# Experts stage: expert outputs with features on partitions, three of four pieces in high and low parts, blocks overlapped, square-root chains per token

## What is computed

```python
q = elu(x @ Wq.T + bq) + 1; k = elu(x @ Wk.T + bk) + 1; v = x @ Wv.T + bv
kv = einsum('nshd,nshm->nhmd', k, v)
z = 1.0 / einsum('nlhd,nhd->nlh', q, k.sum(axis=1) + 1e-6)
ctx = einsum('nlhd,nhmd,nlh->nlhm', q, kv, z)
hs = ctx @ Wd.T + bd + x
attn = (hs - mean(hs)) / sqrt(var(hs) + 1e-12) * gamma + beta
...
top_w, top_idx = top_k(x @ W_gate, 2); combine = one_hot(top_idx) * softmax(top_w)
for e in range(8):
    h = gelu(x @ W_in[e] + b_in[e])            # 128 -> 512
    out = out + combine[..., e, None] * (h @ W_out[e] + b_out[e])   # 512 -> 128
x = x + attn + out
```

## Time and profile before

| | us |
|---|---|
| median of 3 runs | 4531.86 (4531.02 to 4533.04) |
| profiled execution | 4536.7 |
| its span | 4534.8 |
| PE busy | 4234.2 (93%) |
| DVE busy | 3704.0 (82%) |
| ACT busy | 3133.7 (69%) |
| experts_phase | from about 3900 to the end |

### The profile page before, as it was taken

One profiled execution on the slowest core, in us unless ns is written; L12 is line 12 of the kernel. 1 busy time (PEld: TensorE's weight loads), 2 busy tenths in 40 slices (PEclk: granted clock), 3 DMA queues, 4 the chain that ended last, 5 costly groups with the idle time before them and its releaser, 6 DMA issues. The chain is left out here.

```text
span 4534.8 us, 117827 instructions
## 1 busy us (share of the span) xinstructions
PE 4234.2 (93%) x44769; PEld 3395.3 (75%) x44769; DVE 3704.0 (82%) x6460; ACT 3133.7 (69%) x4912; POOL 1783.8 (39%) x965
## 2 busy tenths in 40 slices
PE   6888599999999999999999999999999999599999
PEld 2434278887888878888788887888788888387888
DVE  6888788888888888888888888888888887565553
ACT  5888477777777777777777777777777777243333
POOL 0000155555555555555455555555555554000000
PEclk9999799999999999999999999999999999699999
DMA  2111132232323232322332233322233223100000
GB/s 82 43 43 43 41 69 65 69 72 64 85 68 73 65 83 68 73 68 64 84 73 69 66 68 81 75 67 66 69 81 78 65 65 72 47 8 9 5 7 5
DMA packets 343226, 271.55 MB, mean 60 GB/s; under 512 B 231320, under 2 KB 236064, under 8 KB 341536
## 3 DMA queue, kind: packets, MB, share of 16 engines
q1 hardware_dynamic: 342688, 264.25, 24.3%
HBM read 29.23 MB, written 4.19 MB: 7 GB/s over the span
## 5 line engine op out<-in xcount | busy, mean ns | idle before, releaser
L679 POOL TENSOR_TENSOR qk_rotated<-qk_rotated,rotary_sines 128x1024 f32<-128x1024 f32 x384 | 924.3, 2407 | 1497.7 <-DVE rotary_sines L761 1497.7
L690 POOL TENSOR_TENSOR qk_rotated<-qk_rotated,rnorm 128x1024 f32<-128x1024 f32 x384 | 733.6, 1911 | 7.4
L769 DVE TENSOR_REDUCE qk_sumsq<-qk_squared 128x16 f32<-128x1024 f32 x384 | 465.7, 1213 | 91.7 <-ACT qk_squared L516 91.7
L230 PE MATMUL ps_proj<-qkv_w_hi,x_shifted_hi 128*128 128x512 f32 x1152 | 512.1, 445 | 18.5 <-DVE rotary_sines L761 11.6
L523 ACT ACTIVATE q_t<-ps_qk_t 128x512 f32<-128x512 f32 x384 | 229.7, 598 | 406.5 <-PE ps_qk_t L286 397.6
L751 DVE TENSOR_TENSOR qk_rotated<-ps_proj,rotary_scaled 128x1024 f32<-128x1024 f32 x384 | 467.6, 1218 | 4.5 <-ACT qk_squared L516 4.2
L761 DVE TENSOR_TENSOR rotary_sines<-ps_proj,rotary_scaled 128x1024 f32<-128x1024 f32 x384 | 467.1, 1216 | 1.4 <-POOL qk_rotated L679 1.4
L232 PE MATMUL ps_proj<-qkv_w_hi,x_shifted_lo 128*128 128x512 f32 x1152 | 460.2, 399 | 0.0
L537 ACT ACTIVATE k_t_by_head<-ps_qk_t 64x512 f32<-64x512 f32 x768 | 451.0, 587 | 10.4 <-PE ps_qk_t L295 0.9
L231 PE MATMUL ps_proj<-qkv_w_lo,x_shifted_hi 128*128 128x512 f32 x1152 | 456.4, 396 | 0.0
L311 PE MATMUL ps_scores<-k_t_by_head,q_t 128*32 128x128 f32 x12288 | 415.1, 276 | 9.7 <-ACT ps_scores L546 5.2
(11 more groups left out here) (260 smaller groups left out, 9699.5 us busy)
## 6 DMA issues: line engine op xcount, KB each, us to landing
v_by_window<-v_tokens SPq DMA_DIRECT2D x1152, 128.0 KB, 2.4
v_by_window<-v_tokens SPq DMA_DIRECT2D x384, 64.0 KB, 2.0
k_t_by_head<-k_t_by_head SPq DMA_DIRECT2D x96, 256.0 KB, 4.3
v_by_window<-v_by_window SPq DMA_DIRECT2D x192, 64.0 KB, 2.0
qkv_w_raw<-in_layer_qk_dram SPq DMA_DIRECT2D x7, 1664.0 KB, 9.1
f_k_stacked<-f_k_hi SPq DMA_DIRECT2D x64, 64.0 KB, 2.0
f_k_stacked<-f_k_lo SPq DMA_DIRECT2D x64, 64.0 KB, 2.0
f_q_stacked<-f_q_hi SPq DMA_DIRECT2D x64, 64.0 KB, 2.0
```

The source lines that it names most:

```text
L230: mm(out, hi, HI[:, o:o + 512], start=True, stop=False)
L679: tt(u, u, TB[:], ALU.add).then_inc(added, 1)
L690: tt(u, u, r.unsqueeze(3).broadcast_to((P, 2, 8, DH)), ALU.mult).then_inc(scaled, 1)
L769: nc.vector.reduce_sum(SS[:, 16 * i:16 * i + 16], SQ[:].rearrange("p (h e) -> p h e", e=DH), AX).then_inc(sumsq, 1)
```

## The change

1. Expert output with features on partitions: `expert(i, e, m)` now takes piece m of the 512 hidden features, with w_out stationary and the hidden piece (512 tokens) moving. For m < HS_ = 3 it is three fp32r products of high and low parts; the fourth piece (m = 3) is one fp32 product. ACT makes the high part HHI of each hidden piece one slot later (`high_hidden`), DVE the low part HLO two slots later (`low_hidden`); PE uses piece t four slots later. w_out is split too (WOHI by ACT at t = 14 of block 0, WOLO by DVE in turn 0).
2. The combine weight is now needed along the free axis. CT (8 x 512) is saved to DRAM and read back as eight rows, each broadcast to 128 partitions, into CB, which lies on WI. DVE multiplies (`weigh`, into TMP) and adds (`add`, into Y), both 128 x 512, once per expert. All rows go over SP's queue, one at a time.
3. The bias products are two (KB, slot 5). Y is turned back into tokens by four transposes into VB at t = 7 of the next turn (`tokens_out`), copied by ACT at t = 8 and stored.
4. Turns overlap: pieces 0 and 1 of expert 7 close the turn, 2 and 3 run in slots 2 and 3 of the next one; the last two weightings are at t = 0 and 4 there. `high_x(i + 1)` runs at t = 31. `drain` ends the last turn.
5. Norms: a product with CENT = I - 1/128 centres directly; ACT squares and copies from PSUM; the variance is four products with one column (MCOL), tokens on partitions, so that the 12 steps of the chain work on 128 x 4; DVE multiplies by the identity (`rstd_diag`, 128 x 512) and PE spreads it with a product with ONES. For the second norm W_d and b_d are folded with CENT once at the start (WDC, BDC), and CENT x XN is accumulated under it, in place of the residual. Gamma and beta move to ACT (t = 27), as does q's max (a Relu at t = 10).
6. The combine weights are made in four steps over all chunks in place of eight.

The core of the diff:

```diff
+            def spread_row(i, e):
+                landed, made = held(16 * (E_ * i + e)), held(16 * i + 16)
+                if not isinstance(i, int) or i > 0:
+                    read = held(E_ * (i - 1) + e + 1)
+                    sp.wait_ge(weighted, read)
...
+                after(sp, cb_in, landed)
...
+                sp.dma_start(CB[:, e, :], saved[e:e + 1, :].broadcast_to((P, BLK))).then_inc(cb_in, 16)
...
             with sp.Fori(1, NBLK - 1) as i:
...
+                load_x(i + 1)
+                rows(i, 5, E_)
+                store(i - 1)
+                save_combine(i + 1)
+                rows(i + 1, 0, 5)
...
+            def variance(n):
+                pe.wait_ge(sq, n + 1)
+                for c in range(NT):
+                    last = mm(KV[:, c:c + 1], ZQ[:, chunk(c)], MCOL[:], start=True, stop=True)
...
+            def spread_rstd(n, bank):
+                pe.wait_ge(diag, n + 1)
+                mm(bank[:], ONES[:], DG[:].rearrange("p c d -> p (c d)"), start=True, stop=True).then_inc(spread, 1)
...
+                    mm(G[:], CENT[:], XN[:], start=True, stop=False)
                     pe.wait_ge(ctx_done, i + 1)
-                    mm(G[:], W[:, C_WD:C_WD + P], CTX[:], start=True, stop=True).then_inc(wd_mm, 1)
+                    mm(G[:], WDC[:], CTX[:], start=False, stop=True).then_inc(centered, 1)
...
+            def expert(i, e, m):
+                if m == 0:
+                    after(pe, y_acc, E_ * i + e - 1)
+                if m < HS_:
+                    pe.wait_ge(lo_out, HS_ * (E_ * i + e) + m + 1)
+                    b = e % 2
+                    mm(YB[b][:], WOHI[:, e, m, :], HHI[:, b, m, :], start=(m == 0), stop=False)
+                    mm(YB[b][:], WOHI[:, e, m, :], HLO[:, b, m, :], start=False, stop=False)
+                    last = mm(YB[b][:], WOLO[:, e, m, :], HHI[:, b, m, :], start=False, stop=(m == HM - 1))
+                else:
+                    pe.wait_ge(h_out, SLOTS * i + HM * e + m + 1)
+                    last = mm(YB[e % 2][:], WO[:, e, m, :], HL[:, e % 2, m - HS_, :], start=False, stop=(m == HM - 1))
...
                     if e > 0:
-                        expert(e - 1, m)
+                        expert(i, e - 1, m)
+                    elif m >= 2 and not first:
+                        expert(i - 1, E_ - 1, m)
+                    if t == 5:
...
+                        mm(KB[:], IDENT[:], AT[:], start=True, stop=False)
+                        mm(KB[:], BO[:], CT[:], start=False, stop=True).then_inc(y0_mm, 1)
+                    if t == 7 and not first:
+                        tokens_out(i - 1)
...
-                for c in range(NT):
-                    expert(E_ - 1, c)
-                pe.wait_ge(y_acc, SLOTS * (i + 1))
+                for m in range(2):
...
+                    expert(i, E_ - 1, m)
...
+            def high_hidden(i, e, m):
+                act.wait_ge(h_out, SLOTS * i + HM * e + m + 1)
+                after(act, e_mm, E_ * i + e - 1)
+                a(HHI[:, e % 2, m, :], H[:, m, :], ACT.Copy).then_inc(hi_out, 1)
...
+                    if m < HS_:
+                        after(act, lo_out, HS_ * (E_ * i + e - 1) + m + 1)
...
+                    if t > 0 and (t - 1) % HM < HS_:
+                        high_hidden(i, (t - 1) // HM, (t - 1) % HM)
...
+            def low_hidden(i, e, m):
+                dve.wait_ge(hi_out, HS_ * (E_ * i + e) + m + 1)
+                tt(HLO[:, e % 2, m, :], H[:, m, :], HHI[:, e % 2, m, :].bitcast(F32), ALU.subtract).then_inc(lo_out, 1)
+
+            def weigh(i, e):
+                dve.wait_ge(e_mm, E_ * i + e + 1)
+                dve.wait_ge(cb_in, 16 * (E_ * i + e + 1))
+                after(dve, y_acc, E_ * i + e)
+                tt(TMP[:], YB[e % 2][:], CB[:, e, :], ALU.mult).then_inc(weighted, 1)
...
                     e, m = t // HM, t % HM
+                    if t >= 2 and (t - 2) % HM < HS_:
+                        low_hidden(i, (t - 2) // HM, (t - 2) % HM)
```

More of the change, by code:

```diff
@@ L1585, in _ @@
             tail_sum(q)
[L1588 to L1645, removed]
 def XF2(XF, i):
@@ L1717, in experts_phase @@
[L1717 to L1721, removed]
+        NUM, DEN = KB, VB
+        w_in_s, x_in, x_out, experts_in, cd_in, cb_in = (sem(x) for x in ("weights_in", "x_in", "x_out", "experts_in", "combine_saved", "combine_in"))
@@ new lines, in save_combine, with load_x, store @@
+            def save_combine(i):
+                made, landed = held(i + 1), held(16 * E_ * i)
+                sp.wait_ge(ct_out, made)
+                after(sp, cb_in, landed)
+                sp.dma_start(saved, CT[:]).then_inc(cd_in, 16)
+            def load_x(i):
+                summed = held(i)
+                sp.wait_ge(x1_done, summed)
+                sp.dma_start(XA[:], x_attn[:, i, :]).then_inc(x_in, 16)
+            def store(i):
+                evicted = held(i + 1)
+                sp.wait_ge(yo_out, evicted)
+                sp.dma_start(out[:, i], YO[:]).then_inc(x_out, 16)
@@ new lines, in rows @@
+            def rows(i, a, b):
+                for e in range(a, b):
+                    spread_row(i, e)
+            load_x(1)
+            save_combine(0)
+            rows(0, 0, E_)
+            save_combine(1)
+            rows(1, 0, 5)
+            with sp.Fori(1, NBLK - 1) as i:
+                load_x(i + 1)
[3 more added lines that the diff above has]
+                rows(i + 1, 0, 5)
+            rows(NBLK - 1, 5, E_)
+            store(NBLK - 2)
@@ L1838, in turn, with tokens_out @@
+            def tokens_out(i):
+                pe.wait_ge(y_acc, E_ * i + E_)
+                for c in range(NT):
+                    last = nc.tensor.transpose(VB[:, chunk(c)], Y[:, chunk(c)], IDENT[:])
+                last.then_inc(yt_mm, 1)
+            def turn(i, has_next):
+                first = isinstance(i, int) and i == 0
                 for t in range(SLOTS):
                     e, m = t // HM, t % HM
-                    if t >= 2:
-                        pe.wait_ge(h_out, SLOTS * i + t - 1)
@@ L1855, in turn, with drain @@
-                pe.wait_ge(y_acc, SLOTS * (i + 1))
+                for m in range(2):
+                    if first and m == 0:
+                        pe.wait_ge(w_low, wo_low_count(E_ - 1))
+                    expert(i, E_ - 1, m)
+            def drain():
+                for m in range(2, HM):
+                    expert(NBLK - 1, E_ - 1, m)
+                tokens_out(NBLK - 1)
             pe.wait_ge(w_in_s, 16 * 7)
             pe.wait_ge(setup, NSETUP)
+            mm(G[:, 0:P], W[:, C_WD:C_WD + P], CENT[:], start=True, stop=True)
@@ L1859, in experts_loaded @@
+            mm(G[:, P:P + 1], CENT[:], W[:, C_VEC + CV_BD:C_VEC + CV_BD + 1], start=True, stop=True).then_inc(fold_mm, 1)
+            pe.wait_ge(folded, 2)
             def experts_loaded():
                 pe.wait_ge(experts_in, 32)
-                pe.wait_ge(wi_high, 1)
-            blocks(pe, attention, turn, experts_loaded)
+                pe.wait_ge(w_high, 2)
+            blocks(pe, attention, turn, experts_loaded, drain)
         @block.scalar
@@ L1887, in turn, with tokens_copied @@
+            def tokens_copied(i):
+                act.wait_ge(yt_mm, i + 1)
+                act.wait_ge(x_out, 16 * i + 16)
+                a(YO[:].rearrange("p c d -> p (c d)"), VB[:], ACT.Copy).then_inc(yo_out, 1)
             def turn(i, has_next):
-                act.wait_ge(ln.out, 4 * i + 2)
-                after(act, e_mm, E_ * i)
-                a(XHI[:], XN[:], ACT.Copy).then_inc(x_hi, 1)
+                first = isinstance(i, int) and i == 0
                 for t in range(SLOTS):
@@ L1897, in turn, with drain @@
+                    a(dst, HB[t % 2][:], ACT.Gelu, bias=BI[:, e, m:m + 1]).then_inc(h_out, 1)
+                    if t == 0 and HS_ == HM and not first:
+                        high_hidden(i - 1, E_ - 1, HM - 1)
+                    if t > 0 and (t - 1) % HM < HS_:
+                        high_hidden(i, (t - 1) // HM, (t - 1) % HM)
+                    if t == 8 and not first:
+                        tokens_copied(i - 1)
                     if has_next:
                         attention(i + 1, t)
+            def drain():
+                if HS_ == HM:
+                    high_hidden(NBLK - 1, E_ - 1, HM - 1)
+                tokens_copied(NBLK - 1)
@@ L1899, in _ @@
             act.wait_ge(setup, NSETUP)
             act.wait_ge(w_in_s, 16 * 7)
-            blocks(act, attention, turn)
+            blocks(act, attention, turn, lambda: high_x(0), drain)
         @block.vector
@@ L2072, in first_low @@
                 w_in_low(1)
-            blocks(dve, attention, turn, first_low)
+            blocks(dve, attention, turn, first_low, drain)
 HD1 = D // HEADS
```

347 lines of the change are left out of this document (208 added, 139 removed).

## The result

| | before | after |
|---|---|---|
| median | 4531.44 (4 runs) | 4467.04 (4464.82 to 4469.36, 4 runs) |
| ratio | | 0.9857 (0.984 to 0.9874) |
| profiled execution, span | 4536.7, 4534.8 | 4469.4, 4467.6 |
| b_out load issued (stage start) | 3904.11 | 3899.34 |
| stage start to first hidden product | 62.1 | 48.2 |

64.4 us less, by the medians. In the two profiled executions the stage itself takes 630.7 and 568.3, 62.4 less; the other 4.8 of the spans' difference lie ahead of the stage, in code that is not changed.

What follows compares the result with a forecast made beforehand. PE was taken as the bound mid-turn, with a gap and low clock at the turn's edge. Start 3951.5, turn 0 68, six turns 396 and last turn 54.9 gave 4470.4, minus 64.4: 4467 from the median, range 4442 to 4506.

Steps and rivals of the forecast that it cites:

- The first norm's 10.1: First attention block at the stage's start: its first normalisation takes 10.1 us, where it took 14.7.
- the stretch behind the context 12.2: Stage's start, from the context to hidden product 0: 12.2 us, where it took 24.6.
- the folding 1.6: Stage's start: folding W_d ahead of the first normalisation adds some 1.6 us.
- PE's work without waits: One middle turn without waits: 60.6 us, from 58.3 left of 73.16 plus 1.75 for normalisations and 0.5 for transposes.
- the loop's jump: Jump of the loop in each turn: costs 0.6 us if exposed as in the kernel before.
- The four lined up by hand: PE waits per turn: K and V product 1.1, NUM and DEN 1.2, context (W_d product) 0.9, second spread 0.7; sum 3.9.
- minus 5.0 a turn: Expert products on PE: 28.5 us a turn become 23.5, three of four pieces at 0.69, the fourth at 0.86.
- The gap and the low clock: Turn's edge: overlapping turns remove the 1.84 us gap; low clock and waits behind it go, minus 4.1.
- Rival 2: More waiting: waits twice as long (turn 70, 4493) or one clock fall a turn (6.3 us, 4505); chance 0.22.
- 3 us for a row: SP's queue: each 256 KB broadcast row of combine weights takes about 3 us, hidden; up to 3.8 fits.
- 46 of 61: ACT's work in a turn: 46 of 61 us, so not the bound on average.
- about 48 of 61: DVE's work in a turn: about 48 of 61 us, so not the bound on average.

Runs made afterwards that it cites:

- before_narrow: Kernel before, with the square-root chain's argument and 11 steps on 4 of 512 columns: 4522.2 against 4532.5 (0.9977).
- no_table: Changed kernel with each block's three exps replaced by squares, so no table loads in the turns: 4450.2.
- reorder: Changed kernel with attention steps moved ahead in DVE's and ACT's queues and slot 16's weighting moved to slot 18, nothing added or removed: 4453.2 (0.9827 of before).
- edge_wait: Changed kernel with PE waiting at slot 0 of each later turn for DVE's weighted sum of expert 6, reopening the edge gap: 4485.4.
- chain_wide: Changed kernel with the 11 square-root chain steps after the first over 512 columns instead of 4: 4552.2 (1.0045 of before).

## Why the prediction was right, point by point

The total, 4467 for 4467.04, agreed far better than its parts, and to that extent by luck: the four runs lie between 4464.8 and 4469.4, and in the profiled executions the stage gained 62.4, where 64.4 was added up. The direction and the main path of the gain, PE's work and low clock at and behind the turn's edge, were right.

**The start.** Forecast 3951.5 minus 3966.2, 14.7 less; measured 13.9. The first norm's 10.1 was 10.7, the stretch behind the context 12.2 was 12.6, the folding 1.6 was 1.8. before_narrow puts 10.7 of it on the width of the chain.

**The turns.** 518.9 from the first hidden product to the end was forecast, 520.1 measured. The middle turn, 66.0 forecast, is 65.53, by two errors that cancel. PE's work without waits was put at 60.6, and PE is busy 62.4 (4204.46 to 4269.99). The waits were put at 5.4 and are 3.2; of the 5.4 the terms named, 3.9 and 0.6 for the loop's jump, give only 4.5. The four lined up by hand were 1.1, 1.2, 0.9 and 0.7 and are 1.23, 1.04, 0.49 and 0.40 on average over seven turns (1.19, 0.95, 0.43 and 0.38 in a middle one). What the work term lacks is seen in the turn above: the first product behind a wait takes 1.12 instead of 0.86 (4217.14, 4259.04, 4269.99), the bias product L1869 takes 1.05 without a wait, and the first hidden product behind an attention step takes 0.34 or 0.43 instead of 0.23. The jump of the loop was not seen. Turn 0 took 69.7, forecast 68: PE was at the 1.2 GHz level for 8.5 us of it, worth up to 4.3, where 2 had been put, and it waited 5.4. Turn 1 took 67.1 instead of 66.0: the rows of turn 0 lie on w_in and wait for its low parts, so x came late (DVE waited 1.4 for it), and PE waited 1.8 for its sum there, 0.2 in the middle turns. The last turn took 55.6, forecast 54.9.

**The pieces.** The single costs in the minus 5.0 a turn are right (0.69 and 0.86 stand in the rows), though the third piece made PE's busy time shorter by 7.7 us and not by 10.9. As the price of the third and fourth piece the term is wrong. I took the waits as a sum of their own, independent of the number of parts; they are what the parts cost. In the old order the third piece loses 6.4 us on balance: 7.7 less work, 14.5 more waiting. The waits' place and cause were right (no_table, reorder), their dependence was not worked out.

**The edge.** The gap and the low clock are gone, as forecast. The prediction has the old expert's pieces 2 and 3 in slots 0 and 1 of the next turn; they run in slots 2 and 3, which changed nothing in its sum. That the gap alone sets the low clock is only half right: edge_wait shows the fall at three of seven edges, and short. Rival 2 priced one fall a turn at 6.3 us, from 12.7 us at half speed; the spell in its rows lasted 10.2. Behind the new edge's gap a fall cost 1.7, over the seven edges 0.7 on average. The Trainium skill ("TensorE: Matmul & The Clock Gate", HAM oscillation) has idle gaps between bursts of products send the clock back, and its example has gaps longer than these. Three edges (gaps of 3.0, 2.3 and 2.3 us) show it for shorter ones too; the four others (granted 1.00 behind 2.3, 2.3, 2.3 and 1.6 us of idle) show that it is no rule for a gap of this length. The waits of the changed kernel in turns 1 to 6, at most 1.8 us, never sent it back (granted 1.00 throughout).

**The transfers.** Forecast were 3 us for a row, hidden; it took 3.1, hidden with 0.5 us to spare in the middle turns, and was late once, in turn 1.

**ACT and DVE.** "46 of 61" was 42.5 of 65.5, and "about 48 of 61" was 44.7. chain_wide shows how little such a share says here: 10.6 more us on an engine with 20 to spare cost 11.1 a turn, 7.7 in waits of PE and the rest in the low clock behind them.

## What to carry to other kernels

When engines are coupled every two slots, don't ask whether an engine has time left, but what stands ahead, in its queue, of each step that the bound engine waits for: moving five of DVE's attention steps and ACT's exps forward, and one weighting back, gained 14 us, with nothing removed. Price a long wait of PE with the clock behind it as well: chain_wide was forecast by its waits alone and came 19 us above. An optimisation that shortens the bound engine by giving work to the others (a third split piece) should be timed again after the order is mended, since its sign changed here. A chain of loads behind one another on a queue needs its own budget; put the load that is needed first in front.

## What was not expected of the hardware

The granted clock did not fall reliably. In edge_wait the same 2.3 us of idle, at the same place in five turns, was followed by a spell at 1.2 GHz of 3.4 us twice and by none three times. In chain_wide 2.65 us of idle was followed by such a spell in three turns of six, and 5.3 to 5.7 us by one of 6.8 us each time. An fp32 product 512 wide, 0.86 in a stream, occupied 1.12 when it was the first behind a wait.
